# An attention and FFN kernel on eight cores: four transposes placed around the first v projection, SP's loads and transposes taken in turn, and a new order in the first FFN block and the last tile

## The reference

```python
z = layernorm(x)
q, k, v = z @ Wq, z @ Wk, z @ Wv                   # 64 wide
att = softmax(einsum('bid,bkd->bik', q, k), axis=1)  # over the queries i
x = x + tile(att @ v, (1, 1, 16))
z1 = layernorm(x); z1_prev = z1 shifted by one token
xr = mu_r * z1 + (1 - mu_r) * z1_prev              # xk in the same way, with mu_k
x = x + sigmoid(xr @ W_r.T) * (square(relu(xk @ W_k.T)) @ W_v.T)
```

## Time and profile before

| | us |
|---|---|
| median of 3 runs | 384.51 |
| lowest, highest | 383.32, 384.57 |
| the profiled execution: its own time | 384.74 |
| its span on the slowest core (core 5) | 383.0 |
| spans of all cores | 377.2 to 383.0 |

### The profile page before, as it was taken

The page is one execution under the profiler, slowest core; times in us unless marked ns, Lnnn a source line. Parts: engine busy times, 40 slices in busy tenths (PEclk is TensorE's granted clock), DMA queues, the critical chain, the costliest instruction groups (busy, mean ns, idle before and its releaser), DMA issues.

```text
span 383.0 us, 6327 instructions; the slowest of 8 cores (377.2 to 383.0 us)
## 1 busy us (share of the span) xinstructions
PE 310.7 (81%) x1953; PEld 140.8 (37%) x1953; DVE 220.9 (58%) x438; ACT 232.9 (61%) x360; POOL 109.0 (28%) x158
## 2 busy tenths in 40 slices
PE   0478777777778778776777799989999999999994
PEld 0333332212223434433343344434444444444441
DVE  3687689346234732121249796799379926990045
ACT  1346867987989999999958438312850357022520
POOL 2786637724401888028800003001000000000000
PEclk9998998867695886887559999999999999999999
DMA  7999618999496769995001101422222215130014
GB/s 206 294 326 297 180 67 186 170 305 152 68 166 163 229 195 178 207 183 226 1 3 27 29 0 33 79 110 112 55 56 110 112 27 84 74 147 0 0 56 165
DMA packets 42369, 48.60 MB, mean 127 GB/s; under 512 B 33248, under 2 KB 33504, under 8 KB 41952
## 3 DMA queue, kind: packets, MB, share of 16 engines
q1 hardware_dynamic: 41472, 41.44, 38.3%
q0 software_dynamic: 864, 6.75, 10.5%
HBM read 38.68 MB, written 8.39 MB: 123 GB/s over the span
## 4 chain that ended last, share of the span: by engine, by line
PE 48%; DVE 15%; ACT 13%; issue 11%; DMA 8%; POOL 2%; SPq 1%; DVEq 0%; ACTq 0%; POOLq 0%
PE F L1078 13%; PE F L1059 10%; PE F L1095 10%; DMA xst<-x_in 6%; PE F L891 5%; ACT junkL L1156 5%; ACT Prot L1156 4%; DVE xr L658 3%; PE tf L829 3%; PE tf L868 3%; PE acc L904 2%; ACT junk L1156 2%; DMA z1T<-z 2%; DVE dxk L668 1%; DVE bnst L487 1%
## 5 line engine op out<-in xcount | busy, mean ns | idle before, releaser
L891 PE MATMUL F<-qk 64*128 64x512 bf16 x136 | 59.9, 455 | 30.7 <-ACT junkL L1156 9.3
L1195 ACT ACTIVATE rr<-F 128x1024 bf16<-128x1024 f32 x16 | 16.4, 1025 | 75.9 <-PE F L1059 75.9
L1059 PE MATMUL F<-wr,xr 128*128 128x512 bf16 x256 | 56.5, 379 | 4.0 <-DVE tmp L690 1.4
L1078 PE MATMUL F<-dxk,wk 128*128 128x512 bf16 x256 | 56.1, 379 | 0.3 <-DVE dxk L668 0.3
L1095 PE MATMUL F<-wv,ka 128*128 128x512 bf16 x256 | 55.9, 379 | 0.0
L895 PE MATMUL F<-qk 64*128 64x512 bf16 x120 | 55.3, 474 | 0.0
L1156 ACT ACTIVATE P<-F,negm 128x1024 bf16<-128x1024 f32 (+1 forms) x40 | 37.4, 949 | 10.1 <-PE F L891 5.3
L1156 ACT ACTIVATE Prot<-F,negm 128x1024 bf16<-128x1024 f32 x32 | 39.4, 1364 | 3.9 <-PE F L895 2.6
L1156 ACT ACTIVATE junkL<-F,negm 128x1024 bf16<-128x1024 f32 x32 | 40.2, 1284 | 1.1 <-PE F L895 1.1
L1156 ACT ACTIVATE junk<-F,negm 128x1024 bf16<-128x1024 f32 x32 | 40.1, 1265 | 1.0 <-PE F L895 0.9
L422 POOL TENSOR_SCALAR zst<-xst,nmean,rstd 128x1024 bf16<-128x1024 f32 x32 | 38.0, 1194 | 3.6 <-POOL rstd L412 3.6
(11 more groups left out here) (105 smaller groups left out, 441.9 us busy)
## 6 DMA issues: line engine op xcount, KB each, us to landing
xst<-x_in SPq DMA_DIRECT2D x32, 512.0 KB, 7.0
x<-x_in SPq DMA_DIRECT2D x16, 512.0 KB, 5.9
y_out<-x SPq DMA_DIRECT2D x15, 512.0 KB, 2.6
wr<-wr_in POOLq DMA_DIRECT2D x1, 2048.0 KB, 15.3
wk<-wk_in POOLq DMA_DIRECT2D x1, 2048.0 KB, 18.1
wv<-wv_in POOLq DMA_DIRECT2D x1, 2048.0 KB, 21.1
y_out<-x SPq DMA_DIRECT2D x2, 256.0 KB, 2.2
wqk<-wqk_in POOLq DMA_DIRECT2D x1, 256.0 KB, 9.2
```

The source lines that it names most:

```text
L891: t.matmul(f[:, 0:512], qk2[0:64, kt * 128:(kt + 1) * 128], qk1[0:64, i0:i0 + 512], start=True, stop=True, skip_group_check=True, tile_pos ...
L1059: ins = t.matmul(f[:, hh * 512:(hh + 1) * 512], xr[:, ct, j * 128:(j + 1) * 128], wr[:, ct, hh * 512:(hh + 1) * 512], start=(ct == 0), sto ...
L1078: ins = t.matmul(f[:, dd * 512:(dd + 1) * 512], wk[:, ct, dt * 128:(dt + 1) * 128], dxk[:, q % 2, ct, :], start=(ct == 0), stop=(ct == CT ...
```

## The change

1. **PE and DVE in the attention.** `T(12)` to `T(15)` stood behind `VP2(0)`, close ahead of `QK2(3)`, which reads them. Now `T(12)` and `T(13)` stand ahead of `VP2(0)`, `T(14)` and `T(15)` behind it, and three units of scores stand between `T(15)` and `QK2(3)`. DVE's copies move with them, and the statistics of tile 17 are taken between them.
2. **SP.** `load_x(26)` to `load_x(31)` stood behind the transposes of tiles 18 to 23. Now two transposes and two loads go in turn.
3. **FFN block 0.** The x1 of the fifth tile is computed ahead of the first mix, not behind the second, and its normalization moves ahead of the loading of the sigmoid table. `result(0, 2)` moves ahead of the second half of block 1's mix. ACT normalizes one more tile ahead of `relu_sq(0, 2)`.
4. **The last tile** is computed and stored in parts of 512, 256 and 256 columns, the last in `tf[0]`; it was two parts of 512.

```diff
+        LASTCS = [slice(0, 512), slice(512, 768), slice(768, 1024)]
+        last_f = lambda cs: tf[0][:, 0:256] if cs.start == 768 else f_unit("V", 3, 3)[:, cs]
...
-            turn_z(16)
-            turn_z(17)
-            load_x(24)
-            load_x(25)
-            for i in range(18, 24):
+            for i in range(16, 24, 2):
                 turn_z(i)
-            for i in range(26, TT):
-                load_x(i)
+                turn_z(i + 1)
+                load_x(i + 8)
+                load_x(i + 9)
...
             mx(2)
+            t_evac(12)
+            t_evac(13)
             stats_b(16)
             v_evac(0)
-            t_evac(12)
-            t_evac(13)
-            vt_evac(0)
+            stats_a(17)
             t_evac(14)
             t_evac(15)
-            stats(17)
+            stats_b(17)
+            vt_evac(0)
             stats(18)
...
             ln2_x1(X1SEQ[2])
             ln2_x1(X1SEQ[3])
+            ln2_x1(X1SEQ[4])
             v.wait_ge(P_T2, 2)
...
             mix_r(c_blk(0) + 128, 128, 128, 0)
-            ln2_x1(X1SEQ[4])
...
                         result(q, 0)
                         result(q, 1)
+                        result(q, 2)
                     mix_half(q + 1, 1)
-                for j in range(0 if q else 2, 4):
+                for j in range(0 if q else 3, 4):
                     result(q, j)
...
+                if 4 * q + j == 15:
+                    for cs in LASTCS:
+                        for dt in range(CT):
+                            ins = t.matmul(last_f(cs), ka[:, dt, j * 128:(j + 1) * 128],
+                                           wv2[:, dt, cs],
+                                           start=(dt == 0),
+                                           stop=(dt == CT - 1), skip_group_check=True)
+                        ins.then_inc(P_F, 1)
+                    return
...
+            ln2_apply(4)
             sc.activation(dumb[:, 3:4], dumb[:, 0:1], AF.Sigmoid)
             for q in range(4):
                 for j in range(4):
                     sig(q, j)
-                    if q == 0 and j == 0:
-                        ln2_apply(4)
...
                     ln2_apply(nx[0])
+                    ln2_apply(nx[1])
                     relu_sq(q, 2)
-                    ln2_apply(nx[1])
                     relu_sq(q, 3)
```

More of the change, by code:

```diff
@@ L387, in _ @@
                     t_ = 4 * FBLK[q] + j
-                    for h in range(2 if 4 * q + j == 15 else 1):
-                        cs = slice(512 * h, 512 * h + 512) if 4 * q + j == 15 else slice(0, C)
+                    for h, cs in enumerate(LASTCS if 4 * q + j == 15 else [slice(0, C)]):
                         sy.wait_ge(V_Y, 4 * q + j + 1 + h)
@@ L392, in _ @@
                                      in_=x1[:, t_, cs]).then_inc(D_Y, 16)
-            sy.wait_ge(D_Y, 16 * (TOWN + 1))
+            sy.wait_ge(D_Y, 16 * (TOWN + 2))
         @block.gpsimd
@@ L695, in result @@
                 else:
-                    for h in range(2):
-                        cs = slice(512 * h, 512 * h + 512)
+                    for h, cs in enumerate(LASTCS):
                         v.wait_ge(P_F, 16 + h)
-                        v.tensor_tensor(tmp[:, cs], f_unit("V", q, j)[:, cs], rr[:, j, cs],
+                        v.tensor_tensor(tmp[:, cs], last_f(cs), rr[:, j, cs],
                                         ALU.mult).then_inc(V_TMP, 1)
@@ L952, in _ @@
             QK2(2)
-            scores(2)
+            scores(1)
+            T(12)
+            scores(1)
             SW(2)
             MX(2)
+            T(13)
             scores(1)
             VP2(0)
-            scores(2)
-            T(12)
             scores(1)
-            T(13)
-            VT(0)
-            scores(2)
             T(14)
@@ L966, in _ @@
             T(15)
+            VT(0)
+            scores(3)
             QK2(3)
+            scores(2)
+            SW(3)
             scores(1)
-            SW(3)
             MX(3)
-            scores(2)
             VP2(1)
-            scores(3)
+            scores(4)
             VT(1)
@@ L1089, in V @@
                 f = f_unit("V", q, j)
-                last = 4 * q + j == 15
+                if 4 * q + j == 15:
[7 more added lines that the diff above has]
+                    return
                 for i in range(16):
-                    dt, hh = (i % 8, i // 8) if last else (i // 2, i % 2)
+                    dt, hh = i // 2, i % 2
                     if j == 0 and i % 4 == 0:
@@ L1099, in V @@
                                    skip_group_check=True)
-                    if i == 15 or last and i == 7:
-                        ins.then_inc(P_F, 1)
+                ins.then_inc(P_F, 1)
             def warm(n):
```

## The result

The changed kernel takes 380.25 us (median of 4 runs, 379.18 to 380.85), the kernel before in the same comparison 384.16 us. The ratio is 0.989, 95% interval 0.9855 to 0.9925: 3.9 us faster by the medians. The forecast was 379.4 us. All medians here are of executions in the chip's usual state; two of e1, two of e8 and one of e3 fell in a slower one and are left out.

A forecast was written before the change was run, and what follows sets the result against it. ACT's exponentials bound 94 to 195 us and PE the FFN from 256.7, leaving ACT's 10.9 us idle ahead and the FFN's start. Terms -2.95 - 2.4 + 0.15 = -5.2 us gave 379.4 us against the median, 8-in-10 range 376.6 to 383.2.

The forecast's parts named there:

- The signs named in advance: Trace marks: QK2(3), R(0,3), R(1,1) without waits, ACT's 4.82 us down to about 0.5, QK2(5) waiting about 2 us.
- Part 1: Attention front, transposes T(12) to T(15) moved: 4.82 us of ACT waits go, about 0.5 come back, 4.3 us gained.
- Part 2: SP's queue: moved-up loads delay tile 23 to 78.3 us, so QK2(5) starts only 2.0 us earlier than before.
- the round: SP's queue: two loads and two transposes take 7.0 us, between core 7's 5.6 and core 5's 7.4.
- SW(5): Attention: its wait for a DVE copy falls from 1.46 to 0.5 us, 0.95 us gained.
- Part 3: First FFN block: K and V of block 0 0.9 us earlier, R(1,1)'s wait of 1.44 gone; 2.4 us gained.
- Part 4: Tail: smaller last parts cost 0.35 us more on DVE, the last store saves 0.2; net +0.15 us.
- The sum: Whole kernel: -2.95 - 2.4 + 0.15 = -5.2 us on the profiled execution, 384.74 to 379.5 us.
- A: Rival, SP's queue: rounds take 5.6 us and QK2(5) doesn't wait; -7.3 us, 377.2 us; chance 0.27.
- B: Rival, SP's queue: rounds of 8.3 us take all of the gain back; total -1.25, 383.2 us; chance 0.14.
- C: Rival, SP's queue: rounds above 8.7 us make QK2(5) late and the kernel slower; with 10 us 388.3; chance 0.07.
- D: Rival, FFN: no gain there, later first mixes cost +1.1 us; total -1.7, 382.8 us; chance 0.07.

The follow-up runs named there:

- e1: Changed kernel with SP's queue order of before (loads 26 to 31 behind transpose 23): 379.73 us, ratio 0.9903.
- e8: The changed kernel itself, measured again in a second comparison: 380.52 us, ratio 0.9923.
- e3: Kernel before with only the attention's new PE and DVE order (T(12) to T(15) and their copies): 381.28 us, ratio 0.9961.
- e6: Changed kernel with SP's old queue order and DVE's statistics of tiles 28 and 29 behind the copies for SW(5) and MX(5): 377.40 us, ratio 0.9849.
- e12: Changed kernel, its SP queue kept, with DVE's statistics of tiles 28 and 29 behind the copies for SW(5) and MX(5): 380.74 us, ratio 0.9936.
- e10: Kernel before with only result(0, 2) and block 1's second normalization moved earlier: 186.2 us from the attention's last matmuls to the end, before 187.8.
- e5: Kernel before with only the changes to the first FFN block: 380.13 us, ratio 0.9907.
- e2: Changed kernel with SP's loads 26 and 27 ahead of transposes 22 and 23, loads 28 to 31 behind: 377.76 us, ratio 0.9854.
- e9: Kernel before with only the fifth tile's x1 and normalization moved earlier: 186.3 us from the attention's last matmuls to the end, before 187.8.
- e4: Kernel before with only SP's new queue order: 386.12 us, ratio 1.007.

## Why the prediction was right or wrong

**Direction and size.** Faster by 3.9 us where 5.1 was forecast; the time lies in the range. The signs named in advance came out in kind: waits gone at `QK2(3)`, R(0,3) and R(1,1), a new one at `QK2(5)`, the last operation of 0.42 us. The sizes in the attention did not: ACT's waits fell to 1.6 us and not 0.5, and `QK2(5)` waits 3.86 us on the slowest core and not 2.

**Part 1: the term of 4.3 us was too large; measured 2.2.** This is the step that was mis-sized. Two things were wrong in it. The 4.82 us of the earlier trace rows are core 5's. Core 7 of the kernel before, in the same stretch:

```profile
52.93 1.12 ACT L1156 ACTIVATE P<-F,negm 128x1024 bf16<-128x1024 f32 x1 [1.76 <-PE F L895]
...
56.37 1.12 ACT L1156 ACTIVATE P<-F,negm 128x1024 bf16<-128x1024 f32 x1 [0.94 <-PE F L895]
...
59.63 0.69 ACT L1156 ACTIVATE P<-F,negm 128x512 bf16<-128x512 f32 x1 [0.52 <-PE F L891]
...
62.35 1.12 ACT L1156 ACTIVATE P<-F,negm 128x1024 bf16<-128x1024 f32 x1 [0.17 <-PE F L895]
```

That is 3.39 us, and seven of the eight cores have 3.7 in all from 8 us behind `QK2(2)`'s start to `QK2(4)`. And 1.6 us stay on the changed kernel, not 0.5. So ACT gains 1.8 to 3.2 us here, and e3 gives 2.2 us at `QK2(5)`. POOL began with tiles 16 and 17 earlier, but at 50.64 and not at 49.7: counted from `QK2(2)` this is 3.5 us earlier, not 4.1, and the rest is the later start of this core. So transpose 17 landed at 58.4 instead of 57.3.

**Part 2: the mechanism right, the round short by 0.5 on the slowest core.** There rounds of 7.3, 7.0 and 8.2 us, 7.5 in the mean, stood against 7.0, and the queue began 1.1 us late, so tile 23 came at 80.9 instead of 78.3. Over all eight cores a round takes 7.0 us in the mean, from 6.8 (core 3) to 7.5 (7.2 in e8). What the queue gives back at `QK2(5)` was put at 2.1 us; between e3 and the changed kernel it is 1.3 in the mean, 1.9 in e8 and 2.2 between e6 and e12. `QK2(5)` so starts 0.3 to 0.9 us earlier than before (0.8 to 1.3 against the five executions) and not 2.0. The Trainium skill, "DMA: Bandwidth & Descriptors", section "Where 436 GB/s comes from", was weighed with its figure of 358 GB/s of HBM per core, from which rounds near 5.6 us were estimated; the rows show 7.0 to 8.2, and the core's DMAs moved 191 GB/s in that stretch.

**SW(5): the wait stood for more than it measured.** It was priced at 0.95 us. On core 5 of the kernel before, `QK2(6)` follows `QK2(5)` in 17.68 us, on the other seven cores in 14.2 to 15.3, and in the changed kernel in 14.4 to 15.3. ACT there, behind the wait of 1.46 us:

```profile
85.20 1.12 ACT L1156 ACTIVATE Prot<-F,negm 128x1024 bf16<-128x1024 f32 x1 [1.15 <-PE F L895]
88.03 1.12 ACT L1156 ACTIVATE Prot<-F,negm 128x1024 bf16<-128x1024 f32 x1 [0.53 <-PE F L895]
90.41 1.12 ACT L1156 ACTIVATE Prot<-F,negm 128x1024 bf16<-128x1024 f32 x1 [1.17 <-PE F L891]
92.51 1.12 ACT L1156 ACTIVATE Prot<-F,negm 128x1024 bf16<-128x1024 f32 x1 [0.90 <-PE F L895]
```

3.75 us of idle ACT, where the other seven have 0.4 to 1.3: `MX(5)`, the v projection and its transposes follow with few scores between. It isn't a rate of exchange. Core 7 of e10 (a wait of 1.55 us, 17.84 us from `QK2(5)` to `QK2(6)`) and core 1 of e3 (1.71, 18.09) lost as much, but core 6 of e5 (1.33, 15.23), core 3 of e1 (1.41, 15.22) and core 6 of e2 (1.80, 15.79) lost little. What decides between them stays open.

So on the slowest cores of the two profiles the attention went from 156.1 to 153.3 us, -2.84 against the -2.95 of the prediction, but as +0.5 up to `QK2(5)`, -2.8 from there to `QK2(6)` and -0.5 behind: a right sum from two wrong terms, and so luck. The mean over the cores, which is less at the mercy of one of them, fell by 1.6 and by 0.9.

**Part 3: right, 0.6 us too small.** Forecast 0.9 + 1.44; measured on the slowest cores 1.45 up to V(0,0) and 1.6 at R(1,1), and by e9 and e10 1.5 and 1.6. The delay of R(0,1) is there (1.13 us of waiting); units of R follow each other in 3.45 us (10.52 us for three, the last one's end in it), not in the 3.5 to 3.55 of the steps, and R(0,0) and R(0,1) were held up by less than worked out. This brought back part of what parts 1 and 2 lacked.

**Part 4: right.** From DVE's product of V(3,2) (369.05) to the end of the span (377.6) it is 8.55 us, before 374.58 to 383.0, 8.42: +0.13 against +0.15.

**The sum.** Against the profiled execution -5.4 us (attention -2.84, rest -2.89, the start +0.36), against -5.2 forecast. By the medians it is -3.9: rest -2.8, and about -1.1 left for the attention, in line with its means of -1.6 and -0.9. The profile of before had one core that had lost some 3 us more than the others, and the forecast took that core's waits as what the kernel has to lose in each execution. Of the five executions with the old attention one more (e10, core 7) has such a core; three have none.

**The rivals.** A is out: no core's rounds come to 5.6 us in the mean (6.8 on core 3, which waits only 0.21 us). B is part true: the queue takes back 1.3 to 2.2 us, more than half of part 1's 2.2 to 2.7 though not all. C's mechanism is real without part 1: e4 is slower. D is out by e5.

## What to carry to other kernels

Waits of one core in one execution are not the kernel's: before a wait is taken as the gain, read the same stretch on the other cores, and count what stays in the new order as carefully as what goes. When two transfers of different kind share a queue, changing their order moves the wait to whoever needs the other kind; here it was better to give each kind only the lead it needs (e2), or to go to the consumer's side and put the copy that PE needs ahead of statistics that may wait for a load (e6). The second has a price of its own, 1 us of idle ACT at the next copy. And where cores differ, look at the longest: e6 has the mean of e1 and is 2.1 to 2.3 us faster.

## What the runs showed that was not expected

On core 7 of the changed kernel the second of two DMA transposes behind two loads held SP for 3.2 to 4.5 us in the later rounds, the first 1.3 us, and the two landed after 6.6 to 8.4 us; in a row of transposes each held it 1.2 to 1.3 us and landed after 3.1 (e6). The price falls on the loads behind it as well, which leave later. From the landing of transpose 17 to that of 23 it takes 14.7 us on core 7 of e6 (55.7 to 70.4, one pair of loads between), 18.1 in e2 (56.4 to 74.5, two pairs) and 22.5 in the changed kernel (58.4 to 80.9, three pairs): 3.4 and then 4.4 us for each pair of 512 KB more. That the second pair costs more is this core's: in the mean of the cores it is 14.7, 19.0 and 21.1 us (21.5 in e8), so 4.4 and then 2.0 to 2.5. The 1.05 MB of a pair would take 5.5 us at the 191 GB/s of the changed kernel's stretch, so these numbers don't force a cost of mixing beside that of the bytes; it isn't settled here.

Behind a wait of 1.5 us for a copy on PE, core 5 of the kernel before took 2.8 us longer to `QK2(6)` than the slowest core of the changed kernel; behind waits of 1.3 to 1.8 us on other cores the same stretch took 15.2 to 18.1 us, where 14.1 to 15.4 is usual.
